# A recurrence whose step is cut in two halves of 256 hidden units, on one core of Trainium2

## What is computed

```python
def _mlp(params, z):
    W0, W1, P0, P1 = params
    h = z @ W0 + z @ P0
    h = jax.nn.silu(h)
    return h @ W1 + h @ P1

def step(carry, xs):
    cp, cm = carry                        # parameters and momentum
    k_t, v_t, q_t, a_t, th_t, e_t = xs    # loss: mean((_mlp(params, k) - v) ** 2)
    g = jax.vmap(jax.grad(loss_fn))(cp, k_t, v_t)
    nm = m * e_t - th_t * g               # for each parameter
    np_ = p * (1.0 - a_t) + nm
    out_t = jax.vmap(_mlp, in_axes=(0, 0))(np_, q_t)
    return (np_, nm), out_t
_, ys = jax.lax.scan(step, (cur_p, cur_m), xs)
```

## Time and profile before

| | us |
|---|---|
| median of 3 runs | 12295.05 (12288.87 to 12295.21) |
| the profiled execution | 12288.19 |
| its span, first to last instruction | 12286.5 |
| TensorE busy, share of the span | 79% |
| VectorE busy | 38% |
| ScalarE busy | 16% |
| mean granted TensorE clock | 0.881 |

### The profile page before, as it was taken

The page is one execution under the profiler, slowest core; times in us unless marked ns, Lnnn a source line. Parts: engine busy times, 40 slices in busy tenths (PEclk is TensorE's granted clock), DMA queues, the critical chain, the costliest instruction groups (busy, mean ns, idle before and its releaser), DMA issues. The chain is left out here.

```text
span 12286.5 us, 338221 instructions
## 1 busy us (share of the span) xinstructions
PE 9695.2 (79%) x135922; PEld 5708.6 (46%) x135922; DVE 4669.4 (38%) x11974; ACT 1960.7 (16%) x4398; POOL 232.7 (2%) x167
## 2 busy tenths in 40 slices
PE   5788883523598888888988988889888898896777
PEld 2455551212355555555555555555455555552222
DVE  3444443634723323233233233232332323235555
ACT  1222221211101101011011011110101101012334
POOL 0000000000100000000000000000000000000000
PEclk7999996555898998999999999989898798987888
DMA  2000000143601101011011011120211202020000
GB/s 55 7 7 8 7 8 25 42 123 61 138 17 53 51 18 52 23 47 53 17 53 53 17 53 57 42 81 17 82 45 54 81 17 82 26 72 14 13 10 10
DMA packets 894399, 519.70 MB, mean 42 GB/s; under 512 B 379950, under 2 KB 889462, under 8 KB 892534
## 3 DMA queue, kind: packets, MB, share of 16 engines
q1 hardware_dynamic: 880694, 502.37, 15.1%
q0 software_dynamic: 13312, 12.57, 0.6%
HBM read 323.24 MB, written 154.20 MB: 39 GB/s over the span
## 5 line engine op out<-in xcount | busy, mean ns | idle before, releaser
L2319 PE MATMUL bank<-mv,hdiag 128*32 128x144 f32 x63744 | 2038.0, 289 | 102.1 <-DVE hdiag L2480 102.1
L2319 PEld LDWEIGHTS bank<-mv,hdiag 128*32 128x32 f32 x63744 | 1950.0, 111 | 165.8 <-DVE hdiag L2480 151.2
L2359 PE MATMUL bank<-mvt,ydiag 128*32 128x512 f32 x15936 | 1830.3, 594 | 0.0
L2359 PEld LDWEIGHTS bank<-mvt,ydiag 128*32 128x32 f32 x15936 | 606.5, 109 | 807.8 <-issue 723.1
L2493 DVE TENSOR_TENSOR rep<-bank,wt 128x128 f32<-128x128 f32 x249 | 92.0, 369 | 1863.1 <-PE bank L2319 1863.1
L439 PE MATMUL att_bank<-att_ka,att_qn 128*124 128x496 f32 x1024 | 497.0, 598 | 133.6 <-DVE att_mx L616 67.0
L2423 DVE SCALAR_TENSOR_TENSOR mvt<-mvt,cu,bank 128x256 f32<-128x256 f32 x512 | 223.3, 478 | 791.3 <-PE bank L2254 791.3
L2216 ACT ACTIVATE work<-work 128x128 f32<-128x128 f32 x498 | 142.3, 309 | 2357.6 <-DVE work L2468 2357.6
L2203 ACT ACTIVATE mv<-bank 128x256 f32<-128x256 f32 x1024 | 325.1, 384 | 1091.1 <-PE bank L2267 1091.1
L459 PE MATMUL att_bank<-att_qa,att_ka 128*124 128x248 f32 x2048 | 464.7, 385 | 32.6 <-DVE att_qa L625 32.6
L2254 PE MATMUL bank<-hist,wy 32*128 32x256 f32 x2048 | 393.1, 544 | 90.4 <-DVE wy L2413 89.7
(11 more groups left out here) (402 smaller groups left out, 11450.9 us busy)
## 6 DMA issues: line engine op xcount, KB each, us to landing
hdiag<-between_slopes SPq DMA_DIRECT2D x368, 512.0 KB, 4.6
baset<-between_base SPq DMA_DIRECT2D x265, 128.0 KB, 2.0
between_base<-work SPq DMA_DIRECT2D x256, 128.0 KB
hist<-h SPq DMA_DIRECT2D x1992, 8.0 KB
hist<-y SPq DMA_DIRECT2D x1992, 2.0 KB
hist<-dl SPq DMA_DIRECT2D x1992, 8.0 KB
ct<-between_table SPq DMA_DIRECT2D x184, 128.0 KB, 3.8
between_slopes<-key_zero SPq DMA_DIRECT2D x8, 2048.0 KB
```

What stands on the lines that cost most here:

```text
L2319: mm = e.matmul(psP[32 * j:32 * j + 32, 0:MW], hdiag[:, hf, r, j, :], mv1[:, hf, r, j, :], start=(hf == 0 and r == 0), stop=(hf == 1 and r ...
L2359: mm = e.matmul(psH[32 * j:32 * j + 32, :], ydiag[:, n, j, :], mvt[:, 4 * n + j, :], start=(n == 0), stop=(n == 7))
```

## The change

The steps are built by a function `step(s, last)`; a loop runs it for all but the last step of a chunk, and the last is written out behind the loop, without the parts that belong to a next step. The step of one token now begins in the step before:

- The backward product is two products of half the columns, `back(0, n)` and `back(1, n)`, each of 8 x 4 matmuls with 2 x 128 columns of `mvt`, into two PSUM banks; the history product stands between them.
- VectorE takes the slopes by halves (`slope(hf, ...)`): half 0 behind the first product, then at once x, h and `hdiag` of half 0 for step s+1; half 1 behind the second product, then x and h of half 1.
- TensorE turns half 0 of the new h before the last two n of `back(1, n)`, and half 1 before r = 11 of the first 16 r of the next `pred`.
- ScalarE takes the sigmoids for s+1 at the end of step s. om and sp of a step come at its beginning.
- The replication of sp goes from behind the turn of y to behind `gt`; `ahead(0)` from before Y to behind it, and with it the wait for d's history writes; `ahead(1)` behind the turn of y.
- The three matmuls of WARM are gone.
- W16, W17 and `past` are read from a copy `WC` of `WT` with its two inner dimensions exchanged, made in each update behind the scan "wt" (plus one memset, "tabz").
- SyncE's list is the same; the landmarks that it waits for (h, d) come at other places of a step.

```diff
-                            for j in range(4):
-                                mm = e.matmul(psH[32 * j:32 * j + 32, :], ydiag[:, n, j, :], mvt[:, 4 * n + j, :],
-                                              start=(n == 0), stop=(n == 7))
+                        def back(hf, n):
+                            for j in range(4):
+                                both = mvt[:, 4 * n + j, :].rearrange("p (w f) -> p w f", w=2)[:, :, 128 * hf:128 * hf + 128]
+                                mm = e.matmul(psBack[hf][32 * j:32 * j + 32, :], ydiag[:, n, j, :], both, start=(n == 0), stop=(n == 7))
+                            return mm
...
-                        for k in range(WARM):
-                            e.matmul(b[1][:, HD:], ident[:, :], mvt[:, k, 0:HD], start=True, stop=True)
+                        for n in range(8):
+                            if n == 6:
+                                if last:
+                                    e.wait_ge(T.sem, T.step(c, s, "e"))
+                                    e.nop().then_inc(T.sem, 1)
+                                else:
+                                    turn(0, V.step(c, s, "ha"))
+                            mm = back(1, n)
+                        mm.then_inc(T.sem, 1)
...
                             for r in range(16):
+                                if hf == 0 and r == 11:
+                                    turn(1, V.step(c, s, "h", 1))
...
+                        def slope(hf, names, need):
+                            half, S2, M2 = halves[hf], psBack[hf][:, 0:128], psBack[hf][:, 128:256]
+                            e.wait_ge(T.sem, T.step(c, s, need))
+                            nm(e.tensor_scalar(dh[:, half], S2, W16, None, ALU.mult))
+                            own(st(names[0]))
+                            nm(e.scalar_tensor_tensor(out=dh[:, half], in0=M2, scalar=W17, in1=dh[:, half],
                                                       op0=ALU.mult, op1=ALU.add))
+                            own(st(names[1]))
+                            if hf == 0:
+                                e.wait_ge(T.sem, T.step(c, s, "e"))
+                            nm(e.tensor_tensor(dh[:, half], dh[:, half], psE[:, half], ALU.add))
+                            own(st(names[2]))
+                            if hf == 0:
+                                e.wait_ge(hist_d.sem, c * (hist_d.unit * CH) + s * hist_d.unit)
+                            nm(e.tensor_tensor(dl[:, half], dh[:, half], psR[:, half], ALU.mult))
+                            own(st(names[3]))
+
+                        slope(0, ("dh1a", "dh2a", "dh3a", "da"), "dha")
+                        if last:
+                            e.engine_nop().then_inc(V.sem, 3)
+                        else:
+                            onward(0, s + 1)
+                            e.wait_ge(hist_h.sem, hist_h.step(c, s, "h"))
+                            hidden(0, A.step(c, s, "siga"))
+                            placed(T.step(c, s, "tra"))
+                        slope(1, ("dh1", "dh2", "dh3", "d"), "dhb")
+                        if last:
+                            e.engine_nop().then_inc(V.sem, 2)
+                        else:
+                            onward(1, s + 1)
+                            hidden(1, A.step(c, s, "sig"))
+
+                    with e.Fori(0, steps - 1) as s:
+                        step(s, False)
+                    step(steps - 1, True)
```

More of the change, by code:

```diff
@@ L1818, in __init__, with gap @@
         self.chunk = self.U + CH * self.P
+    def gap(self, name):
+        at = [0] + [self.su[n] for n in self.head] + [self.P + 1]
+        k = self.head.index(name) + 1 if name else len(self.head) + 1
+        return at[k] - at[k - 1] - 1
     def begun(self, c):
@@ L2211, in chunk, with gate, step @@
                             e.activation(bs[:, q % 2, :, :], psBase[q % 2].rearrange("p (a f) -> p a f", a=2), ACT.Copy).then_inc(A.sem, 1)
[L2212 to L2216, removed]
+                    def gate(hf, need):
+                        e.wait_ge(V.sem, need)
+                        half = slice(128 * hf, 128 * hf + 128)
+                        e.activation(sg[:, half], x[:, half], ACT.Sigmoid).then_inc(A.sem, 1)
+                    def step(s, last):
                         e.wait_ge(T.sem, T.step(c, s, "tr"))
@@ L2453, in chunk, with onward @@
                         go(e.tensor_copy(cu[64 * u:64 * u + 64, :, :, :], src), "cu")
[L2454 removed]
+                    nm = lambda ins: ins.then_inc(V.sem, 1)
+                    halves = (slice(0, 128), slice(128, 256))
+                    def onward(hf, t):
+                        nm(e.scalar_tensor_tensor(out=x[:, halves[hf]], in0=dl[:, halves[hf]], scalar=alt[:, bass.ds(t, 1)],
+                                                  in1=xb[:, halves[hf]], op0=ALU.mult, op1=ALU.add))
@@ L2455, in st, with step @@
+                    onward(0, 0)
+                    e.wait_ge(hist_h.sem, c * (hist_h.unit * CH))
+                    hidden(0, A.step(c, 0, "siga", 1))
+                    placed(T.step(c, 0, "tra", 1))
+                    own(V.step(c, 0, "hd0", 1))
+                    e.engine_nop().then_inc(V.sem, V.gap("xz"))
+                    onward(1, 0)
+                    hidden(1, A.step(c, 0, "sig", 1))
+                    def step(s, last):
                         def st(name, back=0):
                             return V.step(c, s, name, back)
-                        nm = lambda ins: ins.then_inc(V.sem, 1)
@@ new lines, in step @@
+                        e.wait_ge(value_in.sem, value_in.upd(c, "first") + s * 16)
+                        nm(e.scalar_tensor_tensor(out=y1[:, :], in0=psP[:, CH:CH + D], scalar=W16, in1=vt[:, :],
+                                                  op0=ALU.mult, op1=ALU.subtract))
+                        e.wait_ge(T.sem, T.step(c, s, "gt"))
+                        nm(e.tensor_tensor(*spread(gdiag, psGT)))
+                        own(st("y1"))
+                        nm(e.scalar_tensor_tensor(out=y1[:, :], in0=psP[:, CH + D:MW], scalar=W17, in1=y1[:, :],
+                                                  op0=ALU.mult, op1=ALU.add))
```

175 lines of the change are left out of this document (83 added, 92 removed).

## The result

The changed kernel takes **11619.99 us** (median of 4 runs, 11607.03 to 11640.99) against 12291.96 for the kernel before (4 runs, 12281.11 to 12295.21): a ratio of 0.9456, 95% interval 0.944 to 0.9473. The forecast was 11621 us, with a range of 11540 to 11800. The profiled execution is the slowest of the four, 11640.99.

What follows compares the result with a forecast made beforehand. The prediction took TensorE to bound the steps, about half the span, with a 3.77 us tail per step. Terms -692 + 10 + 8 = -674 on 12288 gave 11614, plus 7 for the median: 11621 us, range 11540 to 11800.

Steps and rivals of the forecast that it cites:

- the last steps: The 16 steps ending a chunk, where nothing overlaps: +0.63 us each, +10 us in all.
- exits: Fetching the written-out last step in each chunk: 0.5 us for each exit, +8 us, bounds 0 and 6.
- The tail: VectorE and ScalarE chain between history product and next first product: overlapping it by halves removes 3.77 us a step.
- The cut: Backward product in two column halves, 32 groups instead of 16: costs nothing to 0.03 us a step.
- The turns: Two TensorE turns of h inside streams of 32-column products: 0.40 us each, 0.80 a step.
- The stall of half 1: Half 1's chain, turnable at 2.80 us, just meets its cover in the first product: stall 0.05, up to 0.5.
- The table: Reading past with neighbouring elements shortens a VectorE operation on the path: -0.08 us a step, bounds 0 and -0.08.
- Placing half 0: From half 0's turn to the first product: takes 1.01 us against a cover of 1.12, margin 0.1.
- rival B's third mechanism: SyncE's queue makes ahead wait for d's slope writes: 0.3 us, step 22.2, 11852 us; whole rival 0.18.
- The update: The table's extra copy and memset, 0.5 to 1 us, hide under TensorE's 4.96 us DMA wait: cost 0.
- Rival D: The loop's body no longer stays on TensorE and is refetched: 5 to 6 us a step, 12920 us; chance 0.05.
- Rival E: Without filler the granted clock falls to 0.50 within steps: 4200 us more if it held always; chance 0.05.

Runs made afterwards that it cites:

- run 2: Kernel before with the backward product cut into two halves of the columns, one behind the other, nothing overlapped: 12273.39 us (one run).
- run 8: Changed kernel with both turns of h made as four products of 32-column quarters instead of one transposition: 11515.14 us, ratio 0.9391 to the kernel before.
- run 9: Changed kernel with all six 128-column products of a step in 32-column quarters and d's DRAM writes on their own semaphore: 11405.52 us, ratio 0.9311.
- run 4: Changed kernel with the turn of half 1 ahead of r = 12 instead of r = 11: 11585.76 us (one run).
- run 3: Changed kernel with the turn of half 1 ahead of r = 8 instead of r = 11: 11757.39 us (one run).
- run 6: Changed kernel without the copy WC, with W16, W17 and past read from WT as before: 11631.15 us (one run).
- Run 7: Changed kernel with d's four slope writes of a step on their own semaphore, which ahead doesn't wait for: 11575.59 us, ratio 0.9437.
- Run 1: Kernel before with WARM = 0 instead of 3, so without the six filler passes at each step's end: 12721.7 us, ratio 1.0377.
- run 10: Changed kernel with filler products in the updates, at their start and ahead of the base products: 11555.07 us, ratio 0.9429.
- run 11: Changed kernel with all six 128-column products in quarters, d's writes on their own semaphore, and filler in the updates: 11344.79 us, ratio 0.9232.

## Why the prediction was right, by its own steps

**The number** is right, 11620 against 11621, but its parts err to both sides: 233 steps gained 673 instead of 692 us, the last steps with their exits cost 26 instead of 10 + 8. That makes 647 in the profiled executions, where 674 was forecast. The medians differ by 672: the profiled execution is 21 above its median, that of the kernel before 4 below. The coincidence of the last digits is luck, and so are updates that come out even (+1) where executions differ by tens.

**The tail.** All of its 3.77 went. The backward stretch gives 12.09 - 8.78 = 3.31 gained, forecast 3.77 - 0.40 - 0.03 = 3.34.

**The cut** costs 0.04 (run 2; forecast 0.03). The rule of 60 cycles a matmul (the Trainium skill, TensorEngine Tiling (Array Packing), Instruction Overhead), read as an addition, would give an estimate of 0.4: run 2 doesn't show it at 256 columns.

**The turns.** The first product's last pass starts 8.13 behind its first, 7.76 before: one turn is 0.37 (forecast 0.40). What the forecast had no term for is what this is made of (run 8). The Trainium skill, TensorEngine Tiling (Array Packing), Key Properties, says that changing the tiling mode drains TensorE. The traces agree in that a change of form costs time: in the streams' own form a turn costs 0.20 us less (run 8), and the two passes between the backward product's halves 0.37 less (run 9).

**The stall of half 1**, 0.05, is 0 (run 4), and its chain is 2.74 long where 2.80 was summed (run 3). **The table** gives its 0.08 (run 6; 292 ns at L2545). **Placing half 0** was over-sized: it takes 0.81, not 1.01, as the old row holds two turns. I took the whole row as the chain of one.

**What the steady step missed.** With the terms as measured it would be 24.18 - 3.77 + 0.37 + 0.39 + 0.04 - 0.08 = 21.13 us (0.39 is half 1's product with its turn, 3.85, less 16 groups of 0.2165). It is 21.31 in the step shown, and mostly one of two values, 21.31 to 21.35 (79 of the 217 steps that are neither first nor last) or 21.37 to 21.42 (119), as in the one before it:

```profile
6495.56 0.39 PE L2379 MATMUL bank<-mvt,ydiag 128*32 128x256 f32 x1
...
6498.06 1.93 PE L2379 MATMUL bank<-mvt,ydiag 128*32 128x256 f32 x32
...
6499.81 1.05 PE L2393 MATMUL bank<-hist,ddiag 128*32 128x256 f32 x16
```

Half 0's backward product with its two passes of L2385 takes 4.25 here and 4.07 in the step shown, where 3.46 + 0.54 = 4.00 were to be expected of the earlier trace rows; the rest lies just ahead of it, between the old y's products (L2372) and its first pass. That makes 0.2 to 0.3 a step. It isn't a wait for VectorE: the coefficients that L2385 turns are ready at 6496.32, 1.3 us ahead of it (L2569, 0.29 from 6496.03), though their cover is half as long as before. Run 9 shortens that place (3.68), but I haven't tested what causes the difference in the changed kernel; it stays open.

**The last steps** are the term that was mis-sized: +1.6 each instead of +0.63. The prediction had `ahead` meeting the slope writes with 0 to spare and bounded it with 0.3. In the loop that held: 6514.72, no wait (1.2 us in all over the 233 steps). In the steps written out behind it, it doesn't:

```profile
4106.31 6.24 SPq L2082 DMA_DIRECT2D hist<-dl  x8
...
4112.75 1.87 SPq L2188 DMA_DIRECT2D between_slopes<-dl  x4
...
4116.93 0.69 PE L2353 MATMUL bank<-hist,adiag 128*32 128x256 f32 x8 [2.06 <-DMA between_slopes<-dl]
```

Here SyncE's eight history writes take 6.24 us, not 4.87, the slope writes end 1.4 later, and TensorE stands 2.06. The 6.24 is this chunk's alone. What the last steps of the 15 full chunks share is that the slope writes end late, 8.81 to 10.10 into the step (8.59 in the loop): where it is 9.96 or more, in 5 of them, TensorE stands 1.86 to 2.06, in the others 0 to 0.66. So rival B's third mechanism is real, at the last steps. Run 7 takes the dependence away, and the last steps drop by 0.97 to 22.53, the 21.90 of before and the 0.63 that were forecast; that this agrees to the last digit is luck too, as single ones lie between 21.97 and 23.35.

Why is SyncE late there? Code is fetched in just these steps. In steps 2 to 15 the instruction queue q8 moves no packet at all, in the last steps of the full chunks 73 (13 before the change). In the one from 6296.60 to 6319.05:

```profile
q8 instruction: 5, 0.08, 1.7%
```

The kernel before has 1 in that step. And SyncE's issues are stretched when such a packet moves: of its 6972 writes of h, y and d (histories and slopes) 35 take over 0.7 us, where 0.32 (slopes) and 0.56 (histories) are usual, and 30 of the 35 overlap a packet of q8 in time; of the other 6937 only 237 do. That the packets hold SyncE up is so far a coincidence in time, which no run tests by an edit.

**The update** keeps its length as far as can be told, though its cover was nearly used up by something that wasn't foreseen:

```profile
6322.58 0.41 DVE L2436 COPY te<-gates 128x288 f32<-128x288 f32 x1 [3.54 <-issue]
...
6325.25 0.45 DVE L2447 COPY ta<-wt 128x306 f32<-128x306 f32 x1
...
6333.36 1.08 PE L2303 MATMUL bank<-w,ct 64*32 64x256 f32 x8 [1.08 <-DMA ct<-between_table]
```

The copy is 0.45, as taken. But VectorE stands 3.54 us ahead of the update's first copy, waiting for nothing that its row names; in 14 of the 15 updates it is 3.24 to 3.58 (0.41 to 0.43 before). The DMA view shows what comes in meanwhile: in each of these 14 the instruction queue q14 moves a packet 1.2 to 1.5 us behind the end of d, here between 6319.05 and 6323.05:

```profile
q14 instruction: 1, 0.01, 0.9%
```

In the kernel before, the first one comes 8 us or more behind d, or none does. The one update of the changed kernel without such a packet, that ahead of the short chunk, has VectorE standing 0.40. So this is most likely the fetch of VectorE's code for the update; no run takes the fetch away. TensorE's wait for the DMA shrank from the 4.96 of the earlier trace rows to 1.08 (0 to 1.51 over the 15, 1.93 to 4.97 before): in 14 of them it still ends last, so the cost is 0, with a quarter of the margin left, and in one the margin is gone.

**Rival D** didn't happen: in 6441 to 6738, 14 steps of one chunk, the DMA view has no row of the instruction queue q8, and in 6420 to 6440, a chunk's first step, it has

```profile
q8 instruction: 4, 0.07, 1.5%
```

The body is fetched once and kept, as before; it is the written-out last step that is fetched anew in each chunk. **Rival E** was put too low for the wrong reason: I called the remaining idle stretches short without pricing the filler. Run 1 gives the price: had the new order still needed the filler, and lost as much per step as the old one does without it (2.05 us), the time would be 249 x 2.05 = 510 us above, 12130.

## What to carry to other kernels

A chain of small operations at the end of a recurrent step can be hidden by cutting the last large product by columns and letting each half's chain run under the other product; sum each chain link by link from single rows and compare it with its cover. Here half 1's chain came out within 0.1 us, while the placing of half 0, read off a row that holds two operations, was 0.20 off. Filler matmuls aren't idle padding: before taking them out, find what the clock does without them, and put them where long waits remain. Behind a loop, code written out once can meet waits that the loop never shows, and it is fetched again each time, so thin margins need to be checked there too.

## What the runs showed of the hardware

- One product of 128 columns in another form, within a stream of 32-column products, costs 0.37 us, and 0.17 when it has the stream's own form (run 8). Over the six such products of a step the form is worth 0.85 us of 21.37 (runs 8 and 9, less the 0.03 of run 7's edit).
- Behind the loop VectorE stood 3.24 to 3.58 us ahead of its first instruction of the update, in 14 of 15 updates, where it was 0.41 to 0.43 in the kernel before, and each time an instruction packet of q14 came in that pause. The Trainium skill, Runtime: NRT & Kernel Launch, Instruction fetch mechanics, says that a taken branch out of the present window stalls for a fetch; the trace agrees as far as the packets go, but no run here takes the fetch away.
- While q8 fetches code, an issue of SyncE can be stretched from 0.56 to as much as 1.66 us: 30 of the 35 long issues of the changed kernel overlap a q8 packet, and all 12 of the kernel before. Most issues that overlap one aren't stretched (237 of 267 in the changed kernel).
- With filler in the updates their time at 1.2 GHz falls from 1223 to 204 us, and they get 42 to 78 us shorter (run 10). Executions of the changed kernel spread over 34 us; with the filler it was 5 in run 10 and 21 in run 11, so where the spread comes from is open.
